# Layer norms applied by the scalar engine, one low-rank input issued between the decay's column groups, and a new order of steps, in a cross-attention and RWKV block on one core

## The reference

```
# layer 0: cross-attention with 32 query heads on 8 key/value heads of 16
q = x @ Wq + bq;  k = ctx @ Wk + bk;  v = ctx @ Wv + bv
x = LN(softmax(q k' / 4 + mask) v @ Wo + bo + x) * gamma + beta
# layer 1: RWKV time mix
xn = LN(x);  sx = shift(xn) - xn
xxx = tanh((xn + sx * maa_x) @ maa_w1)        # 512 -> 5 x 32
x5[f] = xn + sx * (maa_stack[f] + xxx[f] @ maa_w2[f])      # f = 0..4
w = exp(-exp(time_decay + tanh(x5[1] @ decay_w1) @ decay_w2))   # 512 -> 64 -> 512
r, k, v, g = x5[3] @ Wr', x5[0] @ Wk', x5[2] @ Wv', silu(x5[4] @ Wg')
state = w_t * state + k_t v_t;  out_t = r_t (u k_t v_t + state)
x = x + (groupnorm(out) * g) @ Wo'
# layer 1: channel mix
xn2 = LN(x);  xk, xr = xn2 + shift * maa_k, xn2 + shift * maa_r
x = x + sigmoid(xr @ Wr') * (relu(xk @ Wk')**2 @ Wv')
```

## Time and profile before

| | us |
|---|---|
| median of 3 runs (lowest, highest) | 2467.63 (2464.93, 2467.68) |
| the profiled execution | 2467.93 |
| its span, first to last instruction | 2466.1 |
| TensorE matmuls busy | 2285.7 |
| VectorE busy | 2167.2 |
| ScalarE busy | 941.4 |
| GpSimd busy | 573.0 |

### The profile page before, as it was taken

The page is one execution under the profiler, slowest core; times in us unless marked ns, Lnnn a source line. Parts: engine busy times, 40 slices in busy tenths (PEclk is TensorE's granted clock), DMA queues, the critical chain, the costliest instruction groups (busy, mean ns, idle before and its releaser), DMA issues. The chain is left out here.

```text
span 2466.1 us, 41267 instructions
## 1 busy us (share of the span) xinstructions
PE 2285.7 (93%) x14144; PEld 1568.3 (64%) x14144; DVE 2167.2 (88%) x5337; ACT 941.4 (38%) x3169; POOL 573.0 (23%) x762
## 2 busy tenths in 40 slices
PE   4697999999999999999999999999999999999876
PEld 3374766757676675757667575766757676675643
DVE  1458999999999999999999999999999999999993
ACT  2524262433526243352624335262433526243111
POOL 1122213131221313122131312213131221313100
PEclk8788999999999999999999999999999999999977
DMA  7000001010010101001010100101010010100000
GB/s 253 20 10 11 20 10 38 1 38 10 11 38 10 38 1 39 9 10 38 11 38 1 39 9 11 38 10 38 1 38 10 10 38 11 37 2 27 1 18 9
DMA packets 48415, 61.56 MB, mean 25 GB/s; under 512 B 20208, under 2 KB 25968, under 8 KB 48208
## 3 DMA queue, kind: packets, MB, share of 16 engines
...
## 5 line engine op out<-in xcount | busy, mean ns | idle before, releaser
L1131 DVE TENSOR_TENSOR_SCAN st<-ws,st 128x256 f32<-128x256 f32 x1024 | 624.8, 675 | 10.4 <-POOL st L985 10.3
L842 ACT ACTIVATE probs_or_mixes<-probs_or_mixes,least 128x128 f32<-128x128 f32 x1024 | 396.6, 397 | 25.6 <-DVE least L1078 25.0
L1120 DVE TENSOR_TENSOR st<-bank_pair,kT 128x1016 f32<-128x1016 f32 x256 | 309.7, 1210 | 40.7 <-PE bank_pair L692 38.7
L1141 DVE TENSOR_TENSOR st<-st,rT 128x1024 f32<-128x1024 f32 x256 | 327.2, 1279 | 2.8
L1078 DVE CUSTOM_DVE_ANT_0 probs_or_mixes<-bank,nmask 128x128 f32<-128x128 f32 x1024 | 228.9, 284 | 54.2 <-PE bank L560 32.8
L1015 POOL TENSOR_TENSOR rstd<-rstd,mhalf 128x1 f32<-128x1 f32 x96 | 80.0, 833 | 697.6 <-DVE rstd L1160 697.6
L1009 POOL TENSOR_TENSOR probs_or_mixes<-probs_or_mixes 128x512 f32<-128x512 f32 x160 | 184.8, 1179 | 245.4 <-DVE probs_or_mixes L1203 245.4
L692 PE MATMUL bank_pair<-v_hi,sel 32*128 32x256 f32 x1024 | 183.8, 340 | 48.4 <-DVE st L1120 48.4
L985 POOL COPY st<-s 128x8 f32<-128x8 f32 x256 | 83.8, 340 | 621.1 <-issue 607.6
L842 ACT ACTIVATION_READ_ACCUMULATOR probs_or_mixes<-probs_or_mixes,least 128x1 f32 x1024 | 201.1, 196 | 0.0
L692 PEld LDWEIGHTS bank_pair<-v_hi,sel 32*128 32x128 f32 x1024 | 108.5, 186 | 129.3 <-DVE st L1120 69.0
(11 more groups left out here) (137 smaller groups left out, 4182.4 us busy)
## 6 DMA issues: line engine op xcount, KB each, us to landing
...
wo<-in_wo SPq DMA_DIRECT2D x2, 1024.0 KB, 11.6
...
```

Of the source, the lines that this page charges most:

```text
L842: last = fn(pr[:, n % 4, j, :], pr[:, n % 4, j, :], ACT.Exp, bias=least[:, n, j:j + 1], scale=-1.0, accum_out=rsum[:, n, j:j + 1])
L1120: tt(dst, src, over(kv, DU, 1), ALU.mult).then_inc(outer.sem, 1)
L1131: last = nc.vector.tensor_tensor_scan(v, ws[:, c].rearrange("p b t -> p (b t)"), v, 0.0, ALU.mult, ALU.add)
L1141: tt(v, v, over(rT[:, u // PER, :], DU, 1), ALU.mult).then_inc(weighed.sem, 1)
```

## The change

VectorE's `apply0`, `apply1` and `apply2` are gone; ScalarE has three steps of these names, which compute scale * x + bias with both as columns of 128x1. For that VectorE's `statistics` also writes minus the mean into `less`, and GpSimd multiplies it by the root, in a second instruction that waits for the first. The two small copies that stood in `apply1` and `apply2` become VectorE steps of their own (`row1`, `row2`). The fifth low-rank input leaves `low` and is issued in `tdecay`, between the decay's two halves of 32 columns, so that three column groups are used in turn; its tanh goes from `low` to `tdecay` as well, and `low_rank.4` now waits for `tdecay`. All four orders are new. Group lateness of the first steps changes by one because a period now begins at `low_rank.0`.

```diff
 low:
-                    mm(ps[:, 0:T], w1[:, c, 0:P], x5[:, 3, c], start=c == 0, stop=c == NC - 1)
-                for c in range(NC):
-                    last = mm(ps[64:96, T:2 * T], w1[:, c, P:P + MAA], x5[:, 3, c], start=c == 0, stop=c == NC - 1)
+                    last = mm(ps[:, 0:T], w1[:, c, 0:P], x5[:, 3, c], start=c == 0, stop=c == NC - 1)
 tdecay:
-                    last = mm(ps[0:DEC, 0:T], dw1[:, c, :], x5[:, 0, c], start=c == 0, stop=c == NC - 1)
+                    for r in (0, 32):
+                        mm(ps[r:r + 32, 0:T], dw1[:, c, r:r + 32], x5[:, 0, c], start=c == 0, stop=c == NC - 1)
+                    last = mm(ps[64:96, T:2 * T], w1[:, c, P:P + MAA], x5[:, 3, c], start=c == 0, stop=c == NC - 1)
 scalar:
+            def apply(n, src, dst):
+                def step(g, b):
+                    if n == 2 and b == 0 and known(g + C_AHEAD):
+                        act.wait_ge(filled[XB.of(("turn_c", 1))], XB.through(("turn_c", 1), g + C_AHEAD))
+                    act.wait_ge(pw_n[n].sem, pw_n[n].after(g, b + 1))
+                    fn(dst[:, b, :], src[:, b, :], ACT.Identity, bias=less[:, n, b:b + 1],
+                       scale=rstd[:, n, b:b + 1]).then_inc(ap_n[n].sem, 1)
+                return step
 gpsimd, inverse_root:
-                    tt(v, v, mhalf[:, 0:1], ALU.pow).then_inc(pw_n[n].sem, 1)
+                    tt(v, v, mhalf[:, 0:1], ALU.pow).then_inc(ro_n[n].sem, 1)
+                    pool.wait_ge(ro_n[n].sem, ro_n[n].after(g, b + 1))
+                    m = less[:, n, b:b + 1]
+                    tt(m, m, v, ALU.mult).then_inc(pw_n[n].sem, 1)
 vector, statistics:
+                ts(less[:, n, b:b + 1], aggr[:, n, b, 0:1], -1.0, None, ALU.mult)
-            def apply_norm(g, b, n, src, dst):
-                dve.wait_ge(pw_n[n].sem, pw_n[n].after(g, b + 1))
-                ts(dst[:, b, :], src[:, b, :], aggr[:, n, b, 0:1], rstd[:, n, b:b + 1], ALU.subtract,
-                   ALU.mult).then_inc(ap_n[n].sem, 1)
```

More of the change, by code:

```diff
@@ L120 @@
 PE_ORDER = """
[L121 to L129, removed]
+low_rank.0+1 reduce.5+2 spread.13+2 turn_c.0 turn_c.1 mean.0+2 tdecay.0+1 spread.14+2 low_rank.2+1 proj_r.0+1
@@ L130 @@
+reduce.2+1 score.14 turn_p.11 project.0 turn_m.1+2 turn_p.12 turn_p.13 values.2 reduce.3+1 flip.1 turn_p.14 turn_p.15
+spread.9+1 share.1 values.3 ffn_k.0+2 spread.10+1 project.1 ffn_k.1+2 ffn_r.0+2 spread.11+1 ffn_r.1+2 turn_n.0
+turn_n.1 ffn_v.0+2 ffn_v.1+2 low.0 reduce.4+1 spread.12+1
 """
 ACT_ORDER = """
-turn_c.0 turn_x.0 turn_c.1 decay.0+1 proj_v.0+1 turn_x.1 proj_r.0+1 decay.1+1 mean.1+2 proj_r.1+1 query.0 key.0
-proj_g.0+1 proj_v.1+1 score.0 score.1 score.2 proj_g.1+1 query.1 turn_p.0 turn_p.1 score.3 turn_p.2 score.4 turn_p.3
@@ L135 @@
[L135 to L138, removed]
+turn_c.0 turn_c.1 mean.0+2 tdecay.0+1 proj_r.0+1 proj_v.0+1 turn_x.0 decay.0+1 key.0 proj_k.0+1 decay.1+1 turn_x.1
+proj_r.1+1 query.0 mean.1+2 score.0 query.1 proj_g.0+1 proj_g.1+1 score.1 score.2 turn_p.0 turn_p.1 turn_p.2 score.3
@@ L139 @@
+score.4 turn_p.3 score.5 score.6 score.7 turn_p.4 score.8 turn_p.5 proj_v.1+1 turn_p.6 turn_p.7 apply2.0+2 apply2.1+2
+score.9 proj_k.1+1 turn_m.0+2 flip.0 score.10 turn_p.8 turn_p.9 share.0 score.11 turn_p.10 score.12 score.13
+turn_p.11 score.14 score.15 turn_m.1+2 turn_p.12 turn_p.13 flip.1 turn_p.14 turn_p.15 share.1 apply0.0 ffn_k.0+2
+apply0.1 apply1.0 ffn_k.1+2 apply1.1 ffn_r.0+2 turn_n.0 turn_n.1 ffn_r.1+2 low.0
 """
 POOL_ORDER = """
-rk.0+1 first.1+1 rk.1+1 negate.0 mix.4+1 first.2+1 first.3+1 first.4+1 norm2.0+2 first.5+1 turn_x.0 first.6+1
@@ L145 @@
 """
 DVE_ORDER = """
[L148 to L152, removed]
@@ L153 @@
-score.10 score.11 scan.6+1 score.12 score.13 scan.7+1 gather.0 score.14 outer.8+1 score.15 shift2.0+2 project.0
-inverse.1 weigh.6+1 norm0.0 weigh.7+1 scan.8+1 apply0.0 outer.9+1 gather.1 weigh.8+1 scan.9+1 norm1.0 project.1
-norm0.1 weigh.9+1 apply0.1 keep_row.0 outer.10+1 readout.1+1 apply1.0 norm1.1 outer.11+1 apply1.1 scan.10+1
-weigh.10+1 shift.0 outer.12+1 scan.11+1 scan.12+1 weigh.11+1 ffn_v.0+2 ffn_v.1+2 mix.0 mix.1 outer.13+1 mix.2 mix.3
+weigh.12+2 outer.15+2 scan.13+2 scan.14+2 scan.15+2 proj_v.0+1 weigh.13+2 weigh.14+2 weigh.15+2 outer.0+1 row2.0+2
@@ new lines @@
+scan.0+1 mix.4+1 key.0 outer.1+1 keep_row.0 readout.3+2 scan.1+1 weigh.0+1 weigh.1+1 outer.2+1 score.0 score.1
+var.0+2 scan.2+1 outer.3+1 groupnorm.0+2 proj_g.0+1 scan.3+1 proj_g.1+1 score.2 outer.4+1 score.3 value.0 scan.4+1
+score.4 weigh.2+1 score.5 weigh.3+1 outer.5+1 score.6 score.7 out.0+2 scan.5+1 norm2.0+2 outer.6+1 out.1+2 score.8
+norm2.1+2 weigh.4+1 score.9 weigh.5+1 inverse.0 scan.6+1 proj_v.1+1 outer.7+1 weigh.6+1 score.10 score.11 readout.0+1
+scan.7+1 score.12 score.13 gather.0 outer.8+1 score.14 score.15 scan.8+1 weigh.7+1 project.0 inverse.1 shift2.0+2
@@ L157 @@
+norm0.0 outer.9+1 gather.1 scan.9+1 project.1 norm0.1 weigh.8+1 norm1.0 readout.1+1 outer.10+1 weigh.9+1 norm1.1
+outer.11+1 scan.10+1 row1.0 scan.11+1 shift.0 ffn_v.0+2 weigh.10+1 ffn_v.1+2 weigh.11+1 outer.12+1 mix.0 mix.1
+readout.2+1 outer.13+1 scan.12+1 mix.2 outer.14+1 mix.3
 """
@@ L630, in low_rank @@
                     pe.wait_ge(tanhed.sem, tanhed.after(g, 1))
+                if k == 4:
+                    hold(pe, emptied, g, through("tdecay", 0), (("mix", 8), 0, 0))
                 both = [k, k + 1] if k < 4 else [k]
@@ L1195, in mix @@
                 f = MIX[k]
[L1196 removed]
+                also = {3: [through("tdecay", 0)], 4: [through("tdecay", 0)]}.get(k, [])
                 if k == 4:
```

60 lines of the change are left out of this document (32 added, 28 removed).

## The result

The kernel after takes 2378.02 us (median of 4 runs, 2376.87 to 2385.07) against 2467.27 for the kernel before beside it: a ratio of 0.9646, with a 95% interval of 0.9626 to 0.9666, so 3.5% faster. The prediction said 2415, range 2388 to 2450.

What follows compares the result with a forecast made beforehand. TensorE was taken to bound full periods: -1.7 us (matmuls) and -2.1 (stalls) each, -49.4 over thirteen, -2 for each of two fill periods, +0.8 in the drain, together -52.6 on 2467.9, so 2415 us, range 2388 to 2450.

Steps and rivals of the forecast that it cites:

- What bounds the kernel now: Full periods: TensorE sets the pace, busy 138.6 of 143.0 us, VectorE 4 us behind; in the fill, dependencies do.
- TensorE's sum: Matmul time in low and tdecay: -1.84 and +2.0 for 1.87, so 1.7 us less per period.
- The stalls of before, in the new order: TensorE's idle time per full period: 2.3 us in place of 4.4, with 1.2 of it in named waits.
- four old places: TensorE's stalls after out.1 (0.77), at turn_m.0 (0.56), spread.10 (0.92) and spread.11 (1.32), all said to go.
- The 1.1 added for what the walk would miss: Allowance of 1.1 us of TensorE stalls, added after following both engines through the new orders with trace durations.
- VectorE's sum: VectorE's busy time: six applies go (2.7 us), six negations come (+0.5), net -2.2 us per period.
- The path that the new applies lie on: Norm 1, from project.1's matmuls to turn_n.0: 11.6 us against 11.2 of TensorE work, so turn_n.0 waits 0.6 with handshakes.
- The two of the fill are bound by dependencies; half, -2 each: The fill's two periods, bound by dependencies, each gain about half a full period's saving: -2 us each.
- The slower rival: Layer norm's path decides: turn_n.0 waits 5.3 us, +0.9 per period, 2480 us; chance 0.12.

Runs made afterwards that it cites:

- e16: Kernel after with eight matmuls of the fifth input, read by nobody, put into low: 2407.26 us, ratio 0.9769.
- e4: Kernel after with the row groups that odd and even spreads read exchanged, same work and order: 2384.56 us, ratio 0.9673.
- e9: Kernel after with tdecay's 24 instructions issued one column group after another, not in turn: 2401.93 us, ratio 0.9751.
- e7: Kernel before with nothing but the new orders; applies on VectorE, fifth input in low: 2412.76 us, ratio 0.9790.
- T: Part of the change: the fifth low-rank input and its tanh moved from low to tdecay; alone on the kernel before, 2509.34 us.
- A: Part of the change: the six applies moved from VectorE to ScalarE; alone on the kernel before, 2462.72 us.
- e11: Kernel after with only the last two of the four spread row-group entries exchanged: 2380.82 us, ratio 0.9656.
- e2: Kernel before with only the fifth input moved into tdecay, old orders, applies on VectorE: 2509.34 us, ratio 1.0202.
- e15: Kernel before, old orders, with the fifth input issued twice: unread in low, and in tdecay, where it is used: 2492.02 us, ratio 1.0111.
- e3: Kernel after with the six applies back on VectorE, without the negation and GpSimd's product: 2394.0 us, ratio 0.9713.

## Why the prediction was wrong, step by step

- **What bounds the kernel now**: right. TensorE's sum sets the pace in the new orders (e16: 1.84 us of work cost 2.15).
- **TensorE's sum** is the main step that failed. It put the change of matmul time at -1.7 us per period and measured -3.85. The part it named was right: `low` and `tdecay` together lost 1.85 (2.0 was taken for `tdecay`, 1.86 measured). But it costed only the steps that the diff rewrites, and took every other step at the duration it has alone. The new order gives 32-row steps new neighbours, and neighbours on different rows or columns of the array run side by side (e4, e9): `low_rank.4` with its spread 1.92 instead of 2.39; `spread.5`, `score.4` and `score.6` 2.14 (996.93 to 999.08), where they come to 2.8 one by one. That is another 2.0 us per period, 26 us in all; 1.4 of the 2.0 are at spreads. e7, which has the new orders and not one changed matmul, shows 1.4 of them by itself (137.7 against 139.1); the rest came with T and A. The prediction cited the Trainium skill, "TensorEngine Tiling (Array Packing)", section "Key Properties", for `tdecay` alone; the traces agree that tiles work in parallel, and the same sentence held for the neighbours.
- **The stalls of before, in the new order**: right in sum, less so in its parts. 2.3 us was forecast for what would be left, 2.49 measured, 4.38 before. All four old places went. Of the named new ones `score.2` has 0.35 (0.5), `out.0` 0.60 (0.1), `turn_n.0` 0.80 (0.6). The 1.1 added for what the walk would miss was a guess, and 0.74 of it was found: `proj_r.0` was not named and waits 0.51.
- **VectorE's sum** was put at -2.2 us per period and fell by 1.6 (135.09 to 133.50). e16 says that it doesn't bound.
- **The path that the new applies lie on**: right in size. From the end of `project.1`'s matmuls to `turn_n.0` it was put at 11.6 and is 12.0 (1048.7 to 1060.72). Two errors in it cancel in part. The root of norm 0's second half does stand beside `weigh.8` and takes 1.46, as forecast, and each product takes 0.19 in place of 0.6. But `weigh.9`, held by GpSimd, takes 2.30 (rows in the last section), so that the last statistics start at 1057.22, 1.0 us after their input is there. The slower rival, at 5.3 us for the wait at `turn_n.0`, had the right place and a price over six times too high in the new orders.
- **"The two of the fill are bound by dependencies; half, -2 each"**: the second term that was mis-sized, -16.8 for -4. Of the first period's -15.2 us, 10.9 go with the clock: of TensorE's busy time in it, 44.1 us of 121.7 lay in stretches at half clock before, and 22.2 of 106.1 after, and half of the 21.9 between them is time. Another 4.7 is less work: `reduce.4` and `spread.12` went behind `low` (about 2.2, which the drain gets), and the savings of a full period. Idle time rose by 0.4. The forecast had no term for the clock here. Why the clock comes up sooner was not tried, and not all of it need come from the orders: the same figure is 12.4 in e7, but 30.2 in e11, which differs from after in two row assignments alone and has a first period 3.6 us longer. So this part of the cause stays open.
- **A term left out: the clock.** The prediction took 1.00 for every full period. Two of the thirteen of before last 145.43 where the others last 143.5, and each has a stretch of 3 to 4 us at a low clock. (A third has one too and is no longer than the rest: the wait of 1.32 at `spread.11`, which follows, is gone in it.) In one of the two it stands behind the wait of 0.77 of the earlier trace rows, which is 0.42 to 0.43 in eleven of the other twelve periods, in the other behind a wait of 1.67 at `spread.11`:

```profile
1198.00:1200.00 2.00, 1.23 (x14) 0.80 (x10) 1.97 (x5) 1.85 (x9) 0.00 (x0) 1.00 0.00 0
1200.00:1202.00 2.00, 2.00 (x8) 1.51 (x7) 1.82 (x5) 0.00 (x0) 1.13 (x2) 0.63 0.00 0
1202.00:1204.00 2.00, 2.00 (x6) 1.62 (x5) 2.00 (x17) 0.00 (x0) 0.66 (x1) 0.51 0.00 0
1204.00:1206.00 2.00, 2.00 (x14) 1.77 (x14) 1.45 (x5) 0.47 (x1) 0.00 (x0) 1.00 0.03 8
```

  In this change it is worth only 0.3 us per period, since before has two such periods and after none; 0.1 of it is lost again, as a few periods of after are up to 0.4 longer at full clock. It is what separates e2 from e15. In e3 it makes four of thirteen periods 1.5 to 1.9 us longer, 6.7 in all. So of the 17.8 us that A takes off the thirteen periods of e3, 6.7 are a clock that stays up, and 11.1 are shorter periods at full clock (138.68 to 137.83), half of it in work and half in waits.
- **The parts as independent terms**: the sum gave T a fixed value. It is worth -33, -19 or +45 us by the order around it. The forecast for the change as a whole didn't suffer by it.

The sum put right: per period -3.85 (matmuls) -1.9 (stalls) -0.2 (clock) = -5.95, times 13 = -77; fill -16.8; first `low` +2.0; drain +0.9; together -91.
